# One core, 16 sequences: another order for the three passes over a score tile, and one tile per step on every engine

## The reference, cut to what matters

```python
for i in range(6):                                   # token stage
    a, g = split(conv1d(x, conv_w[i]) + conv_b[i]);  x = (a * sigmoid(g) + x) * 0.7071
attn1 = softmax(q1 @ k1.T / 4)                       # 8 heads of 16, 1024 x 1024 each
attn2 = softmax(q2 @ k2.T / 4)
# of windows of 4 query rows: mean, std, maximum and minimum of attn1 and attn2
hid = relu(gate_in @ gw1 + gb1);  hid = relu(hid @ gw2 + gb2)
alpha = sigmoid(hid @ gw3 + gb3)
out = ((alpha * attn1 + (1 - alpha) * attn2) @ v) @ Wo
# feed-forward: layernorm, linear, eight expert slices with gelu, linear, gelu
```

## Time and profile before

| | us |
|---|---|
| median of 3 runs | 6310.05 (6308.97 to 6312.23) |
| the profiled execution, first to last instruction | 6310.3 |
| PE busy, DVE busy, ACT busy | 5419.2, 5358.7, 5292.3 |
| POOL busy | 2425.1 |
| mean granted TensorE clock | 0.927 of 2.4 GHz |

### The profile page before, as it was taken

The page is one execution under the profiler, slowest core; times in us unless marked ns, Lnnn a source line. Parts: engine busy times, 40 slices in busy tenths (PEclk is TensorE's granted clock), DMA queues, the critical chain, the costliest instruction groups (busy, mean ns, idle before and its releaser), DMA issues.

```text
span 6310.3 us, 127411 instructions
## 1 busy us (share of the span) xinstructions
PE 5419.2 (86%) x34070; PEld 2706.4 (43%) x34070; DVE 5358.7 (85%) x6524; ACT 5292.3 (84%) x9997; POOL 2425.1 (38%) x4629
## 2 busy tenths in 40 slices
PE   6988889889888888889889888888889888898886
PEld 4443434444343443434444343443434444343443
DVE  2888888898988888888898888888889888888883
ACT  2888888889888888888889888888888888888884
POOL 6424343342433424343342433424344242433422
PEclk8999989999998999989999898999999999898997
DMA  1001010010101001010010101001010010101000
GB/s 37 19 20 26 19 28 19 20 27 22 26 19 28 19 20 26 18 28 19 20 27 22 26 19 28 18 21 26 18 28 19 20 26 22 25 19 27 19 22 12
DMA packets 165102, 142.52 MB, mean 23 GB/s; under 512 B 89197, under 2 KB 108269, under 8 KB 164141
## 3 DMA queue, kind: packets, MB, share of 16 engines
q1 hardware_dynamic: 159100, 124.09, 8.5%
q0 software_dynamic: 4352, 8.92, 0.7%
q10 hardware_dynamic: 816, 0.02, 0.0%
HBM read 21.26 MB, written 8.91 MB: 5 GB/s over the span
## 4 chain that ended last, share of the span: by engine, by line
PE 40%; issue 22%; DVE 18%; ACT 14%; POOL 3%; ACTq 1%; SPq 1%; DMA 0%; DVEq 0%; POOLq 0%
PE ps_w L387 18%; PE ps_s L387 8%; DVE negmax L717 7%; PE ps_t L387 7%; ACT junk L580 7%; PE ps_o L387 6%; DVE rowmin L723 4%; ACT exps L587 4%; DVE o_t L732 1%; DVE bn L742 1%; ACT hpre L636 1%; DVE mean_all L736 1%; DVE recip L735 1%; PE ps_w L435 1%; SPq L329 1%
## 5 line engine op out<-in xcount | busy, mean ns | idle before, releaser
L723 DVE TENSOR_REDUCE rowmin<-ps_s 128x1 f32<-128x1024 f32 x2048 | 2479.1, 1221 | 559.8 <-ACT junk L580 468.0
L580 ACT ACTIVATE junk<-ps_s,negmax 128x1024 bf16<-128x1024 f32 x2048 | 2300.9, 1124 | 473.2 <-DVE negmax L717 438.2
L717 DVE TENSOR_REDUCE negmax<-ps_s 128x1 f32<-128x1024 f32 x2048 | 2412.9, 1215 | 156.0 <-PE ps_s L387 128.1
L587 ACT ACTIVATE exps<-ps_t 128x512 f32<-128x512 f32 x4120 | 2265.7, 615 | 230.7 <-PE ps_t L387 211.8
L387 PE MATMUL ps_s<-kst,qst 96*128 96x512 bf16 x4096 | 1329.3, 408 | 486.7 <-DVE rowmin L723 421.0
L387 PE MATMUL ps_t<-qst,kst 99*128 99x512 bf16 x4120 | 1442.9, 408 | 220.6 <-ACT exps L587 165.7
L387 PE MATMUL ps_w<-xc,cw 128*128 128x256 f32 x4704 | 1253.5, 404 | 22.0 <-ACT ug L656 12.4
L387 PE MATMUL ps_o<-exps,v_cur 128*32 128x256 f32 x16512 | 1161.6, 401 | 20.4 <-POOL v_cur L1012 20.3
L387 PEld LDWEIGHTS ps_w<-xc,cw 128*128 128x128 f32 x4704 | 902.8, 199 | 354.2 <-issue 117.2
L387 PEld LDWEIGHTS ps_t<-qst,kst 99*128 99x128 bf16 x4120 | 414.8, 101 | 1120.9 <-ACT exps L587 877.0
L871 POOL TENSOR_SCALAR ctmp<-ug 128x256 f32<-128x256 f32 x408 | 165.9, 407 | 1569.0 <-ACT ug L656 1561.0
(11 more groups left out here) (179 smaller groups left out, 4147.6 us busy)
## 6 DMA issues: line engine op xcount, KB each, us to landing
qst<-part SPq DMA_DIRECT2D x1542, 32.0 KB, 2.0
kst<-part SPq DMA_DIRECT2D x1542, 32.0 KB, 2.0
qst<-mrow SPq DMA_DIRECT2D x1028, 1.5 KB
out_dram<-z SPq DMA_DIRECT2D x17, 512.0 KB, 3.2
fc1s<-in_fc_w SPq DMA_DIRECT2D x17, 256.0 KB
fc2s<-in_fc_w SPq DMA_DIRECT2D x17, 256.0 KB
cw<-in_conv_w SPq DMA_DIRECT2D x1, 2304.0 KB
att<-in_table,idx POOLq DMA_INDIRECT x136
```

Of the source, the lines that this page charges most:

```text
L580: nc.scalar.activation(junk[:, n % 2, :], ps_s[:, n % 2, :], ACT.Exp, bias=negmax[:, r, t:t + 1], accum_out=sumsq[:, r, t:t + 1]).then_inc ...
L587: nc.scalar.activation(exps[:, n % RING, 512 * c:512 * c + 512], ps_t[:, c, :], ACT.Exp, scale=0.5).then_inc(s_exp, 1)
L717: nc.vector.tensor_reduce(negmax[:, r, t:t + 1], ps_s[:, n % 2, :], axis=AX, op=ALU.max, negate=True)\
L723: nc.vector.tensor_reduce(rowmin[:, r, t:t + 1], ps_s[:, n % 2, :], axis=AX, op=ALU.min)\
```

## The change

- `squares(n)` waits for `row_min(n)`, `row_min(n)` no longer waits for ACT, and `scores(n)` waits for `squares(n - 2)`.
- All three engines take one step per turn: PE scores, weighted, scores_t, tasks; ACT exp_t, tasks, squares; DVE row_max, row_min, tasks.
- `exp_t` is one instruction of 128x1024 over both banks of `ps_t`, and `scores_t(n)` waits for all of tile n - 1. `s_exp` and `s_st` count tiles instead of halves.

```diff
@@ scores, scores_t, weighted @@
-                pe.wait_ge(s_min, i * STEPS + n + 1)
+                pe.wait_ge(s_sq, i * STEPS + n + 1)
...
+                pe.wait_ge(s_exp, i * STEPS + n + 1)
                 for c in range(2):
-                    pe.wait_ge(s_exp, i * (2 * STEPS) + 2 * n + c + 1)
-                    mm(ps_t[:, c, :], kst[:, u % RING, P * t:P * t + P], qst[:, u % RING, 512 * c:512 * c + 512])\
-                        .then_inc(s_st, 1)
+                    last = mm(ps_t[:, c, :], kst[:, u % RING, P * t:P * t + P],
+                              qst[:, u % RING, 512 * c:512 * c + 512])
+                last.then_inc(s_st, 1)
...
-                    pe.wait_ge(s_exp, i * (2 * STEPS) + max(2 * n, 1))
+                    pe.wait_ge(s_exp, i * STEPS + max(n, 1))
@@ PE's loop @@
-                for n in range(0, STEPS, 2):
+                for n in range(STEPS):
                     scores(i, n)
+                    weighted(i, n)
                     scores_t(i, n)
-                    scores(i, n + 1)
                     for tk in STEP[n]:
-                        task("body", i, tk)
-                    scores_t(i, n + 1)
-                    weighted(i, n)
-                    weighted(i, n + 1)
-                    for tk in STEP[n + 1]:
                         task("body", i, tk)
@@ squares, exp_t @@
-                act.wait_ge(s_max, i * STEPS + n + 1)
+                act.wait_ge(s_min, i * STEPS + n + 1)
...
-                for c in range(2):
-                    act.wait_ge(s_st, i * (2 * STEPS) + 2 * n + c + 1)
-                    nc.scalar.activation(exps[:, n % RING, 512 * c:512 * c + 512], ps_t[:, c, :], ACT.Exp,
-                                         scale=0.5).then_inc(s_exp, 1)
+                act.wait_ge(s_st, i * STEPS + n + 1)
+                nc.scalar.activation(exps[:, n % RING, :], ps_t[:, :, :].rearrange("p c q -> p (c q)"), ACT.Exp,
+                                     scale=0.5).then_inc(s_exp, 1)
@@ ACT's loop @@
-                for n in range(0, STEPS, 2):
+                for n in range(STEPS):
                     exp_t(i, n)
-                    squares(i, n)
                     for tk in STEP[n]:
                         task("body", i, tk)
-                    squares(i, n + 1)
-                    exp_t(i, n + 1)
-                    for tk in STEP[n + 1]:
-                        task("body", i, tk)
+                    squares(i, n)
@@ row_min, DVE's loop @@
-                dve.wait_ge(s_sq, i * STEPS + n + 3)
...
-                for n in range(0, STEPS, 2):
-
+                for n in range(STEPS):
                     row_max(i, n)
-                    row_max(i, n + 1)
+                    row_min(i, n)
                     for tk in STEP[n]:
-                        task("body", i, tk)
-                    row_min(i, n)
-                    row_min(i, n + 1)
-                    for tk in STEP[n + 1]:
                         task("body", i, tk)
```

More of the change, by code:

```diff
@@ L366, in _ @@
                     if j:
-                        sp.wait_ge(s_st, i * (2 * STEPS) + 2 * (T * (j - 3) + T - 1 + LAG_T) + 2)
+                        sp.wait_ge(s_st, i * STEPS + T * (j - 3) + T + LAG_T)
                     else:
-                        sp.wait_ge(s_exp, i * (2 * STEPS) + 2)
+                        sp.wait_ge(s_exp, i * STEPS + 1)
                     settle()
@@ L679, in _ @@
             act.sem_inc(s_sq, 2)
-            act.sem_inc(s_exp, 2)
+            act.sem_inc(s_exp, 1)
             act.sem_inc(s_mrow, 64)
@@ L830, in _ @@
             last.then_inc(s_init, 1)
-            dve.sem_inc(s_min, 2)
             dve.sem_inc(s_out, 16)
```

## The result

| | before | after |
|---|---|---|
| median, us | 6309.51 (6308.49 to 6312.23, 4 runs) | 6119.45 (6117.17 to 6125.02, 4 runs) |
| ratio | 1 | 0.9699, 95% interval 0.9686 to 0.9713 |
| profiled execution, first to last instruction | 6310.3 | 6115.3 |
| mean granted TensorE clock | 0.927 | 0.950 |

A forecast was written before the change was run, and what follows sets the result against it. No single engine was the bound: PE, DVE and ACT, nearly equally busy, wait for each other. Terms -42 + 21 + 0 + 3 + 2.7 + 4 = -11 us per sequence, times 16 = -178, gave 6135 us, range 5960 to 6440.

The forecast's parts named there:

- DVE's 58 us of losses: DVE's loss per sequence before the change: 34.7 us idle before minima, 8.1 before maxima, 15.1 in reductions without overlap.
- lost overlap: DVE's reductions hold 305.7 us per sequence, where 256 in a row at 1.135 each would take 290.6.
- Quiet steps, -42: Maximum and minimum in a row on DVE: a pair falls from 5.20 to 4.54 us, 42 us less per sequence.
- the ring: A half of `ps_s` goes round in two steps, from scores to release by `squares`: 4.33 us against DVE's 4.54.
- PE's tasks, +21: PE's tasks stand before the next scores: convolutions cost 16.8 us, `fc2` 3.0, `fc1` 1.4, together 21 more per sequence.
- The merged exponential, 0: ACT's exponential as one instruction: holds ACT 0.95 us like two halves, so 0, within 0.05 either way per tile.
- The drain, +3: PE waits about 0.9 us for DVE's transpose of `ps_o`; hidden except where a task follows, 3 us more per sequence.
- POOL's chain, +2.7: DVE waits for POOL before `mrow`, 3 us at step 8: +2.1 there and +0.6 at step 120, per sequence.
- Single events, +4: After stops (gelu, table loads) PE runs at the lower clock: about five stops at 0.8, 4 us more per sequence.
- The task in front of `squares`: Slower rival: ACT's activation before `squares` waits for PE's task and delays release of `ps_s`; 6400 us, chance 0.25.
- Convolutions absorbed: Faster rival: the tile in hand smooths out most of PE's convolutions, 21 falls to about 6; 5890 us, chance 0.12.
- No change: Rival: PE and ACT stand in line for one tile, rings close at 2.6 us, not 2.27; 6310 us, chance 0.07.

The follow-up runs named there:

- e1: The changed kernel with the exponential in two halves of 512 again, each waiting and released by itself: 6118.97 us, ratio 0.9700.
- e13: e4 with DVE's transpose for the drain of `ps_o` put in front of that step's minimum instead of behind it: 6102.12 us, ratio 0.9678.
- e4: The changed kernel with POOL's two late `msplit` tasks (units 1 and 15) put ahead of the `qk` task before them: 6106.79 us, ratio 0.9678.
- e6: The changed kernel with ACT's tasks moved behind `squares` instead of in front of it: 6671.32 us, ratio 1.0571.
- e11: The changed kernel with PE's tasks of step n moved behind the scores of step n + 1, ACT left as it is: 7290.01 us, ratio 1.1424.
- e3: The kernel before with only the new dependence and DVE taking maximum and minimum together, its pairs of steps kept: 7097.68 us, ratio 1.1252.
- e10: The changed kernel with the old order of passes (maximum, squares, minimum; scores wait for the minimum): 9311.99 us, ratio 1.4758.
- e7: The changed kernel with only the middle one of three taps of every convolution, so its output differs: 5970.13 us, ratio 0.9465.

## Why the prediction was right, and where it was not

The time was 15 us off, and the sum per sequence was -11 against -10.85 in the traced one. That the second pair is so close is luck: the mean of 15 sequences is -12.4, so the sum was 1.4 too small per sequence. The steps:

**What bounds the kernel.** Three engines that wait for each other: held. DVE's 58 us of losses were made up partly wrongly: the 15.1 us of "lost overlap" came from a group's busy time, 305.7 against 290.6. After the change the same two groups hold 311.7, though DVE idles less. A group counts the overlap of two of its own rows once, and two maxima in a row overlap; a maximum and a minimum are in different groups. So this figure says how reductions are arranged, not what is lost. Both groups taken as one, the reductions cover 303.1 us before and 298.5 after: against 290.6, 12.5 were lost and 7.9 still are.

**Quiet steps, -42.** They run at 2.26 to 2.28 us, as worked out from the ring. But the pair that gave the 5.20 was no quiet pair; it holds a convolution and an `attw` task. Pairs without any PE task, the first of a sequence apart, took 4.81 to 4.97 before and 4.61 to 4.71 after. What had 5.2 to 5.4 and came down to 4.53 were the pairs with `qk`, `embT`, `e2h` or `nT`, about 0.7 each.

**PE's tasks, +21.** 15.5 us in 39 convolution steps where 16.8 stood for 44, with another split: 21 of the 39 take about the full 0.57 above 2.27 (0.5 was taken, for 18) and the others 0.20 on average (0.3). `fc2` 2.98 where 3.0 stood, `fc1` 0.8 where 1.4 stood.

How these two terms meet is seen by kind of pair. The forecast credits every pair with 0.66, and then charges:

| pairs | by the forecast's terms | measured, traced sequence |
|---|---|---|
| 29 with a convolution | -19.1 + 16.8 + 1.4 = -0.9 | -1.8 |
| 18 without | -11.9 + 3.0 (`fc2`) = -8.9 | -7.4 |
| 17 at stops | -11.2 + 4 + 2.7 = -4.5 | -1.6 |
| the drain, in all kinds | +3 | |

Calling a pair of 5.20 quiet was an error of the reading, but the convolutions were charged against the same 4.54 that it was credited to, so it went out again where it was largest. That the two cancel was not argued in the forecast and is luck in part. What it left are the pairs without a task, 4.81 to 4.97 and not 5.20.

**The merged exponential, 0.** Right (e1), for a reason the text gave only in part: its cover is not just ACT's slack, it also starts later. Where the next activation follows without a gap, a whole exponential holds ACT for 0.92 us and two halves for 0.95 (medians, changed kernel and e1), inside the bounds of 0.05. The estimate by the Trainium skill (ScalarE: Activation LUTs, "What ACT_TABLE_LOAD costs") of 0.09 us per tile has the right sign and is somewhat large: the busy time is 142.5 us less over 2060 tiles, 0.07 each. At the end nothing arrives.

**The drain, +3.** PE waits 135.5 us in 144 times, 0.94 each, as the 0.9 said, and e13 shows that nothing is to be had by shortening it.

**POOL's chain, +2.7.** The wait at step 8 is 2.80 us (3 was said), at step 120 1.01:

```profile
2725.74 0.21 DVE L752 STREAM_TRANSPOSE mrow<-mparts 128x32 bf16<-128x32 bf16 x1 [2.80 <-POOL mparts L906]
...
3046.49 0.21 DVE L752 STREAM_TRANSPOSE mrow<-mparts 128x32 bf16<-128x32 bf16 x1 [1.01 <-POOL mparts L906]
```

What it is worth was mis-sized: e4 takes it away and gains 13 us, 0.8 per sequence. The text had the loads follow `mrow`, and nobody wait for them. At the end of a sequence they follow POOL's last `qk` task, and PE waits for them, so POOL's chain counts there and not only through `mrow`.

**Single events, +4.** The first gelu costs what it did (6.50 before), and the tile behind it is late as well:

```profile
2931.83 1.23 DVE L708 TENSOR_REDUCE negmax<-ps_s 128x1 f32<-128x1024 f32 x1 [6.72 <-PE ps_s L387]
...
2937.07 1.23 DVE L708 TENSOR_REDUCE negmax<-ps_s 128x1 f32<-128x1024 f32 x1 [2.88 <-PE ps_s L387]
```

The lower clock behind stops was charged as a loss, and behind one it came no more: after the third layer norm, the convolution of step 50 took 2.77 us before, behind a wait of 3.23 us on PE; now PE waits 1.69 us there and the convolution takes 1.46. That pair went from 7.64 to 4.86 us. Before:

```profile
2932.12 1.04 PE L387 MATMUL ps_s<-kst,qst 96*128 96x512 bf16 x2 [3.23 <-DVE rowmin L723]
...
2934.66 2.77 PE L387 MATMUL ps_w<-xc,cw 128*128 128x256 f32 x6
```

After:

```profile
2841.95 0.60 PE L387 MATMUL ps_s<-kst,qst 96*128 96x512 bf16 x2 [1.69 <-ACT junk L576]
...
2843.49 1.46 PE L387 MATMUL ps_w<-xc,cw 128*128 128x256 f32 x6
```

The pair at step 44 went from 7.43 to 5.87 us the same way (its convolution took 2.54 and takes 1.46). The pair at step 116 went from 7.13 to 5.67, but not by the clock: its scores take 0.60 us in both kernels. Against them stand losses of 1.2 to 1.5 us at step 8, behind the second gelu and at the loop's end, in the traced sequence (0.65, 1.27 and 0.49 on average of 15). So the term hides gains and losses larger than itself; it was right in size only as their balance.

**The rivals.** The task in front of `squares` does not decide against the change: e6 shows that it is the better place, by 552 us, for ACT's wait and for PE's next task together. The chain behind this rival was drawn correctly as a chain of hand-overs, but ACT would have waited for the minimum all the same, and that was left out. Its loop is real one edit away (e11). "Convolutions absorbed" is refuted by their 2.84 us. "No change" fell with the 2.26 us of the quiet steps.

Open stays how much of the loss in e3, e6 and e10 is the lower clock (0.897, 0.933 and 0.796, against 0.950), and how much the waiting itself; no run held the one and changed the other.

## What to carry to other kernels

When three engines share two buffers, draw the loop that each order closes, and count how many steps it has to go round in: the same work gave 6119, 6278, 6671, 7290 and 9312 us by order and waits alone, and the halves of a good change were each bad (e3, e10) because each closed a loop that the other opens. Put work that needs nothing new, such as the second reduction or the task's activation, where its engine would wait in any case. And price each kind of step by itself, in pairs taken from the trace, before multiplying one pair by 64.

## What the runs showed that was not expected

- A removed wait often only changes its name. e4 took 42 us away and gained 13, e13 took 96 away and gained nothing that can be told from that; e7, which took work from PE in steps that PE sets, did gain (9.6 of 15.5 us per sequence by the steps, 9.3 by the measured time).
- At the end of a sequence POOL's chain counts a second time: in 12 of 15 sequences of the changed kernel, and in all 15 in e4, the next one's first scores wait for loads that follow POOL's last `qk` task.
- The mean granted clock is no measure of the time: 0.927 before and 0.950 after, 0.897 in e3 and 0.796 in e10, but 0.925 in e11, at 1.14 times the time, and 0.914 in e7, the fastest, which gives PE less to do. A stop of PE of 3.23 us was followed by a convolution at half speed, one of 1.69 us at the same place was not.
- A reduction of 128x1024 from PSUM lasts 1.22 us, but in a row one starts every 1.13 to 1.14 us whether it reads the same tile or another; a gap of 0.48 us in front of one costs the step 0.57.
